# A two-layer macaron kernel: earlier weight loads in borrowed buffers, a halved broadcast, and a new order table

## What is computed

```python
x = x + 0.5 * _L0_ffn_ref(_layernorm(x), ...)   # silu(gate) * up, then down; int32 weights minus 128, hidden 704
x = x + _L0_attn_ref(_layernorm(x), ...)        # 16 heads of 16, rotary, causal softmax, output projection
x = x + 0.5 * _L0_ffn_ref(_layernorm(x), ...)
x = x + 0.5 * _L1_ffn_ref(_layernorm(x), ...)   # sigmoid(x1) * x2; weights rounded to -1, 0, 1 by mean(abs(w))
x = x + _L1_attn_ref(_layernorm(x), ...)        # 16 query heads on 4 key heads, ALiBi bias, causal softmax
x = x + 0.5 * _L1_ffn_ref(_layernorm(x), ...)
```

## Time and profile before

| | before |
|---|---|
| median of 3 runs | 582.63 us (580.01, 582.63, 582.76) |
| profiled execution | 580.01 us, its span 578.3 us |
| PE busy | 531.4 us |
| DVE, ACT, POOL busy | 460.7, 400.1, 341.1 us |
| DMA moved | 31.75 MB, mean 55 GB/s |

### The profile page before, as it was taken

How to read it: one execution, slowest core, us unless ns; L and a number is a source line. 1 busy time by engine, 2 the same in 40 slices (tenths; PEclk the granted TensorE clock), 3 DMA queues, 4 the chain that set the end, 5 groups by cost and what they waited for, 6 DMA issues and landing times.

```text
span 578.3 us, 12694 instructions
## 1 busy us (share of the span) xinstructions
PE 531.4 (92%) x4924; PEld 291.1 (50%) x4924; DVE 460.7 (80%) x813; ACT 400.1 (69%) x605; POOL 341.1 (59%) x427
## 2 busy tenths in 40 slices
PE   2885987998999999999999999999999999999997
PEld 1352643544564564555546455465465644554664
DVE  4799779998799779589986988878898677884453
ACT  5883557597567849766597775878668686679533
POOL 2367858882896687854456284365462845246544
PEclk9997988999999999999999999999999999999999
DMA  8700101121112001130100120010211002111201
GB/s 329 315 2 0 38 18 56 56 75 28 34 70 82 25 16 38 41 116 15 61 21 3 62 76 2 21 49 11 69 41 37 6 22 88 41 38 41 76 36 37
DMA packets 20524, 31.75 MB, mean 55 GB/s; under 512 B 7360, under 2 KB 8768, under 8 KB 20312
## 3 DMA queue, kind: packets, MB, share of 16 engines
q1 hardware_dynamic: 20464, 30.94, 15.2%
HBM read 13.75 MB, written 2.36 MB: 28 GB/s over the span
## 4 chain that ended last, share of the span: by engine, by line
PE 57%; DVE 15%; POOL 6%; ACT 6%; SPq 5%; issue 5%; DMA 4%; DVEq 0%; POOLq 0%; ACTq 0%
PE PS L584 16%; PE PS L608 10%; PE PS L695 10%; PE PS L675 5%; PE PS L626 5%; PE PS L660 4%; DVE MX L1049 4%; PE PS L710 3%; ACT PB L837 3%; DMA MASKM<-maskm 2%; PE PS L568 2%; SPq L519 2%; PE PS L642 2%; PE PS L540 2%; POOL PB L1153 1%
## 5 line engine op out<-in xcount | busy, mean ns | idle before, releaser
L837 ACT ACTIVATE PB<-PS 128x1024 f32<-128x1024 f32 x160 | 157.7, 1023 | 44.4 <-PE PS L675 40.7
L1049 DVE TENSOR_REDUCE MX<-PS 128x2 f16<-128x1024 f32 (+2 forms) x192 | 157.1, 864 | 18.4 <-PE PS L540 18.0
L584 PE MATMUL PS<-XT,WGU 128*128 128x512 f16 x660 | 158.4, 384 | 4.3 <-DVE DS L1010 2.8
L1125 POOL TENSOR_TENSOR HH<-TH,HH 128x512 f16<-128x512 f32 x71 | 83.1, 1185 | 68.5 <-ACT HH L805 68.5
L1153 POOL TENSOR_SCALAR_AFFINE_SELECT PB<-PB 128x512 f32<-128x512 f32 (+1 forms) x140 | 73.0, 551 | 64.6 <-ACT PB L837 64.4
L584 PEld LDWEIGHTS PS<-XT,WGU 128*128 128x128 f16 x660 | 59.7, 98 | 79.9 <-issue 8.2
L608 PE MATMUL PS<-WD,HH 128*128 128x256 f16 x660 | 77.5, 273 | 0.9 <-POOL HH L1125 0.6
L695 PE MATMUL PS<-PB,V 128*32 128x512 f32 (+3 forms) x1024 | 75.5, 435 | 1.2 <-POOL PB L1153 1.0
L608 PEld LDWEIGHTS PS<-WD,HH 128*128 128x128 f16 x660 | 62.3, 98 | 13.3 <-issue 2.6
L660 PE MATMUL PS<-SK,SQ 63*128 63x256 f16 (+3 forms) x512 | 59.5, 300 | 7.7 <-DVE MX L1049 3.7
L805 ACT ACTIVATE HH<-TH 128x512 f16<-128x512 f32 (+1 forms) x86 | 52.2, 627 | 18.5 <-DVE TH L992 7.0
(11 more groups left out here) (115 smaller groups left out, 751.9 us busy)
## 6 DMA issues: line engine op xcount, KB each, us to landing
SQ<-QPB SPq DMA_DIRECT2D x24, 256.0 KB, 2.5
OC<-OT SPq DMA_DIRECT2D x16, 256.0 KB, 2.4
RB<-scratch SPq DMA_DIRECT2D x64, 64.0 KB, 2.3
SK<-QPB SPq DMA_DIRECT2D x12, 256.0 KB, 2.4
SQ<-MT SPq DMA_DIRECT2D x128, 1.0 KB
out<-X SPq DMA_DIRECT2D x8, 256.0 KB, 2.2
PB<-gu SPq DMA_DIRECT2D x2, 704.0 KB, 6.1
LATE<-gu SPq DMA_DIRECT2D x2, 704.0 KB, 13.8
```

The lines of the kernel that those rows point to most:

```text
L584: m = e.matmul(o[:, :], WGU[l][:, k, col:col + P], rows_of(f)[j][:, k, :], start=j == 0 and k == 0, stop=j == 1 and k == 1)
L837: e.activation(PB[Q % 2][:, j, :, :], two_banks("s", i), ACT.Exp, scale=0.25).then_inc(a_exp, 1)
L1049: e.tensor_reduce(mx[:, :, pr, t], o[:, :, col:col + (t + 1) * P], AX.X, ALU.max, negate=True).then_inc(a_max, 1)
L1125: e.tensor_tensor(hh[1][:, s * T:(s + 1) * T], value_of(j)[0], hh[0][:, s * T:(s + 1) * T], ALU.subtract).then_inc(f_lo, 1)
```

## The change

Six edits come together.

1. LATE is gone. Its contents lie in SQ[1] and SK[1], the stacked tiles of the odd attentions, which are not needed before attention 1.
2. SP issues the layer-1 FFN weights (wd1, then gu1) ahead of batches 2 and 3 of x, the rotary table and the masks.
3. ACT's last four `k` steps (which fill SQ[1] and SK[1]) wait for the end of w14.
4. `R` is two DMAs of 128 KB (the even and the odd partitions) where it was four of 64 KB.
5. The builder's default replaces `dynamic_dma_scratch_size=256`.
6. All five strings of `ORDER` and `banks` are new. Each string has the same letters as often as before.

```diff
-        LATE = sb("LATE", [P, 2, 4 * T])
...
-        late = [LATE[:, k, :] for k in range(2)]
+        late = [t[1][:, :, :].rearrange("p h t -> p (h t)").bitcast(F32) for t in (SQ, SK)]
...
             e.dma_start(BO[:, :], bo1).then_inc(l_a0, 16)
+            e.dma_start(rd[0], wd1[:, 0:4, :]).then_inc(l_w3, 16)
+            e.dma_start(rd[1], wd1[:, 4:, :]).then_inc(l_w3, 16)
+            for k in range(2):
+                e.dma_start(rgu[k], gu1[:, k, :]).then_inc(l_w1, 16)
             e.dma_start(X[:, 2 * NT:, :], x_in[:, 2 * NT:, :]).then_inc(l_x23, 16)
             e.dma_start(ROPE[:, :, :], rope).then_inc(l_c2, 16)
             e.dma_start(MASKW[:, :, :, :], maskw).then_inc(l_c2, 16)
             e.dma_start(MASKM[:, :, :, :], maskm).then_inc(l_c2, 16)
-            e.dma_start(rd[0], wd1[:, 0:4, :]).then_inc(l_w3, 16)
-            e.dma_start(rd[1], wd1[:, 4:, :]).then_inc(l_w3, 16)
-            for k in range(2):
-                e.dma_start(rgu[k], gu1[:, k, :]).then_inc(l_w1, 16)
...
                     src = scratch[n % 2, u].rearrange("(a g s) t -> a g (s t)", a=4, g=2)
-                    for a in range(4):
-                        e.dma_start(RB[32 * a:32 * a + 32, u, :], src[a].unsqueeze(0).to_broadcast([16, 2, T])).then_inc(t_si[u], 16)
+                    for g in range(2):
+                        e.dma_start(RB[g:P:2, u, :], src[:, g, :].unsqueeze(1).to_broadcast([4, 16, T])).then_inc(t_si[u], 16)
...
                     w.wait_ge(l_c2, 48)
+                    if z == 1:
+                        w.wait_ge(p_dve, 30)
...
     "sp":
-        "kkrkrrkDrSrRDSRrrDkkSrRrDSRrrkDrSlkRDSRrkrkrDrrSlRDSRrkkrrDSrDRSrRrkkrDrSRDrSRrDrkkSRrDSRrrOODrSRDSR"
+        "kkrrkrkrDSrRDSRrkrDSRkrrDSRrrDrkSRkDSRrrlkkrDrSRrDSlRrkrkDrSRrDSrRrkkrDrSRDrSRrDrkrkSRDrSRrrrDSRDOSOR"
```

More of the change, by code:

```diff
@@ new lines @@
+        "smsgssmGspmsgsmGmmpsmsmsmgssGmmmpsmsvsvmssmuummmpqqsoooossddssmqmqpsmttdmsdssmgggsGGgpmmgsmGsmssmmgs"
+        "GmmmGpmssvvsmuudsddmdsqmsqoopmottossmgsqsmgmggGGGsgmspmsmgGssGqttpssdgsssdgddGgpgGgmvmmmgmvGuGmuGmoo"
+        "oomqmsqsmsqdmmsdmdsmdmssmmspmssmmsmsttspgssmggmGgGgsmGGgGmspsmstddtddmssggmpmvmgGguusGGsqgsmqsmgGsqm"
+        "sGoomspmmddddmsmsoomspmmttsssggGssGsgmmpsmgGmsgmsmGgGmpmsvsmssmmmdddmsdsspsmsttomogmsguguooGqqqsGmms"
+        "gmGsGggGmspsmmmddmsdssmdmsspsmmssmmspttvsmmgggGgGGgGgGsmmssttssddddooommmopspuusmgqsmqqssggGsGsspssm"
@@ new lines @@
+        "gmmmGpmgvmmgGmGmsmtsmsstsmmpdddmsdooosmgsosmsmgGgGmsmpmsgssGsgsgsspssGGttpddgddgGgGgGggGGoooodddttdg"
+        "ggGgGGgGGgdddd",
+    "dve":
+        "NwNtthwwhwkhwhwhtwthwwNhhwwdwNdwhnhwhkuuhtpqptqdwdpqhnpqhhkuuhhhpqttqpmmmmmxmmmspqsmhpmqxhmdmsmmdmxm"
+        "mkmhsmhnmxsmhmmmcmmxsmmmhmcxmmumummpqpoqoxNmqdppmqmtcmtdmsxhnskhsshmmmmhmmsxshmmhmmcuxumdmdNpqmqopmt"
+        "tomxNhmmphqhkmhmmxhhtqptcshsddnkhsshcmsmmmmhsumxhuhmoommllmlmxmdmmdmmxNmmmmmttNxmhchkhmhmhmhxmdttdmn"
+        "mssmhmsckuuhxhshmlsmhslmhmlomxmddmNmmmoxmttNhchmmkmhhmxmhmhmmmcxmmmdmdnmttmmxshusuoohlklslhmmmxshshs"
+        "mhmmmdmcxmdmNmmmmNttmcxmhhkhhhhmmtxdtdnommomNuumlmxhllchkhmmmmhmxmmhmmmhcxmmtmtdmdomxhomNmhkmmhmxhch"
+        "httcddhhkhhhhooNXtthdkhhhhhddd",
@@ new lines @@
+    "act":
+        "TwwXxxwttthXtthxxhhwhtwhkttwwwthwhXtkhwxthYwyyhthXxkQQvtkthQtvYQtyytthhxxhhQTkQkktthkeeeteeQeeQhhoee"
+        "eteeeoetehhhoeeeteeYoeevecveeyyhcoeQeQeeeXoexxQeQetetehttohheeetheteYohcehveeyvyeeceXoxxQeeeetttQhXe"
+        "hehttoheeethQxhxoeeetQteechtothhtvYtyvchyhhQeQeeQeeeeeoeeXexxeeoeetthththetXhtheheoexxceettoYhtvyyet"
+        "ehQetQhetechehhQeoeeXoexxeeetteeehhteothetehhtXhoeveeeceeecoexxeYteytyhtQQhQeehtetthehheoeeeeeoeeeXe"
+        "oxxecXttvhhtththhteheexexceYeooyyetQXeQQeetteheeoeethothvhthceeeeexhoxceeteeetthXhehoteeeeheeteteeho"
+        "hxxotthchthtcthhthXxxthttthhhthth",
@@ new lines @@
+        "7246102742462135643560256460362350162460642104630516247620432064715640624057216052416204346023406472"
+        "0420620460246024762174026503273462154260264124340631426402635402705402602752406320634613624036024623"
+        "4604750260420720542056024104640264062047142426204672064073410315706426147205674214624064124624606240"
+        "6206450126402375421376024603264060162406314625420760256027024206526045621640365026402605620735207604"
+        "702460362720462412062742043047672650476143571367262737530657065431",
```

43 lines of the change are left out of this document (10 added, 33 removed).

## The result

| | before | changed |
|---|---|---|
| median of 20 runs each, on the same chips | 580.82 us (578.52 to 582.76) | 583.84 us (582.37 to 585.89) |
| ratio to before, 95% interval | | 1.0054 (1.0041 to 1.0066) |
| profiled span | 578.3 us | 584.2 us |

A forecast was written before the change was run, and what follows sets the result against it. PE was taken as the bound, busy 531.4 of 578.3 us. Start -4.5, R +1.5 and other order 0 gave -3.0 us: 577.0 against the profiled execution, 579.6 us against the median; range 573.5 to 587.5 us.

The forecast's parts named there:

- The start, -4.5: Up to the first scores: they come at 86 to 87 us, not 90.8, gaining 4.5 us (between -1 and -6).
- 2.0 us at w13 from the wait for x: In DVE's start: its 2.98 us wait for x is filled with wd1 sums, 2.0 us kept at w13 (0 to 2.98).
- PE's wait of 6.5 us still there: Sign for the start: PE still waits 6.5 us, but the wait ends near 56 us.
- The gain travels to the end unless the order wastes it: After the start: with no DVE slack up to 200 us and none on PE later, the 4.5 us reach the end.
- R, +1.5 (0 to 8.4): R transfers POOL waits for: on four DMA engines each lands about 1.2 us later, costing 1.5 us in all.
- two prices: Cost of one R, estimated from two transfer rows: 13.8 or 11.0 engine-us, so 2.8 to 3.4 us on four engines.
- Rival B: R transfers: R spreads over 16 engines and lands 1.2 us earlier, -8.1 us in all, 574.5 us; chance 0.10.
- A: R transfers decide: all POOL waits for R pass on, plus four moved c, +8.7 us, 591.3 us; chance 0.12.
- The rest of the tables. I take 0, between -3 and +4: Order from 200 us on and the tail: most steps move one or two places, taken as 0 us.
- Rival D: From 200 to 550 us: the new order doubles PE's idle time, +8.0 -3.0, 587.6 us; chance 0.10.
- Rival C: First 200 us: 3 us of the start's gain is lost again after 91 us, 581 to 583 us; chance 0.24.

The follow-up runs named there:

- e3: The kernel before with the new loads, buffers, ACT wait and strings only up to the first scores, old strings behind, old R: 577.35 us, 0.9923 of before.
- e15: The kernel before with the new loads, borrowed buffers, ACT's wait and scratch size, all old strings and the old R: 1.0119 of before, 6.9 us slower.
- e4: The kernel before with its old start and old R, but the new strings behind the first scores: 1.0111 of before, 6.5 us slower.
- e13: e12 with one more change, the transposes t18 write PSUM bank 0 and not bank 2: 582.55 us in a single run, made for its trace.
- e12: The changed kernel with the old four-transfer R and one ACT exponential moved ahead of a norm near 350 us: 1.0015 of before.
- e14: The changed kernel with the old R and t18 in PSUM bank 0, ACT's exponential left behind the norm: 583.20 us in a single run, for its trace.

## Why the prediction was wrong

*The start, -4.5: right in size, by a sum whose terms were partly wrong, so in part luck.* It is 4.5 us in e3's median (2.8 to 6.2), first scores and first maximum within 0.7 us of the forecast. But I had 2.0 us at w13 from the wait for x and nothing from POOL's moved steps. The rows of the changed kernel:

```profile
49.15 0.57 DVE L952 TENSOR_SCALAR SQ<-SQ,GS 128x704 f16<-128x704 f32 x1
49.64 0.58 DVE L952 TENSOR_SCALAR SK<-SQ,GS 128x704 f16<-128x704 f32 x1
50.14 0.94 DVE L956 SCALAR_TENSOR_TENSOR WGU<-SQ,GS 128x704 f16<-128x704 f32 x1
51.00 0.94 DVE L956 SCALAR_TENSOR_TENSOR WGU<-SQ,GS,SK 128x704 f16<-128x704 f32 x1
```

w13 starts 2.35 us later than before and is done 2.3 us earlier: 2.8 us instead of 7.45. I had read in the earlier trace rows that POOL's 3.46 us step stood there, and that the change moves it away, without asking what it did to the DVE step beside it. It is the order and not the new buffers: in e15, with the new buffers and the old order, w13 takes 7.46 us (53.22 to 60.68), as before. No run moves POOL's steps alone, so how much of the 4.5 us they bring is not measured. "PE's wait of 6.5 us still there" was wrong too: PE's longest wait between 20 and 60 us is 2.9 us, at 30.8.

*"The gain travels to the end unless the order wastes it": right.* e3 shows the first half and e4 the second.

*R, +1.5 (0 to 8.4): mechanism right, somewhat small.* Four engines, +0.8 us each on the mean in the old order (expected 0.7 to 1.3), 1.9 to 2.5 us at the end. Of its two prices one was misread: the row of 0.43 for 2.00 us holds 196 KB (98 GB/s) of the 262 that an R moves. The other, 11.0 engine-us from a transfer whose row is whole, held: the changed kernel's R takes 0.23 x 16 x 3.20 = 11.8. Rival B is out (share 0.23), and so is A.

*"The rest of the tables. I take 0, between -3 and +4": the step that failed.* It measured +5.1 us in the changed kernel (3.2 to 7.0) and +6.5 (4.8 to 8.1) behind the old start, both above its upper bound of +4, though the first interval reaches below it. With it at zero the forecast was -3.0; with +5.1 the same sum gives +2.1, and with R at 2.5 the measured 3. It was the term without a row behind it: I wrote that most steps move by one or two places, and took small moves for harmless, though the same prediction says that with 8.0 us of idle in 350 "a new order can mostly lose there". Rival D named this with 0.10, and called for 5.9 us of new idle; in the trace there are 4.3, 3.8 of them without the new R. The order at 350 us, and the bank that `t18` shares with `p17`, stood in the two tables beforehand. What is shown is that the strings behind the first scores lose it, and in which four stretches; the step by step cause is shown for one wait of 1.09 us, and stays open for the rest.

*Rival C (lost from 91 to 200 us): small.* The changed kernel loses 2.1 us between 115 and 193 us, but e3 with the old order loses 1.6 there too, and still ends 4.5 us ahead by the medians.

## What to carry over

When an order changes as a whole, split it at a point where both versions have done the same work, and time each part under the other; here a gain of 4.5 us and losses of 5.1 and 2.5 showed as one small difference. Ask what each joint costs by itself. Give no zero to reordered steps in a stretch where the bounding engine is full: count which of its waits are 0.2 to 0.5 us now, and look who frees the PSUM bank of each moved step. In a DMA, look at the outermost count of both sides before merging transfers: here half the issues left a quarter of the engines.

## What the runs showed of the hardware

**A DVE step held up by POOL.** With the new buffers and the old order (e15), DVE and then POOL:

```profile
53.22 0.59 DVE L951 TENSOR_SCALAR SQ<-SQ,GS 128x704 f16<-128x704 f32 x1
53.72 3.43 DVE L951 TENSOR_SCALAR SK<-SQ,GS 128x704 f16<-128x704 f32 x1
```

```profile
53.31 3.46 POOL L1089 TENSOR_TENSOR WA<-OT,WA 128x1536 f16<-128x1536 f32 x1
```

Two equal DVE instructions take 0.59 and 3.43 us. The first began before POOL's, the second ends 0.4 us behind the end of POOL's step of 3.46 us (56.77). In the changed kernel the same two take 0.57 and 0.58, with nothing longer than 1.46 us on POOL; there POOL's big step stands at 30.11 us and takes 3.11. A profile counts such a held step as busy time of DVE, not as a wait. The Trainium skill ("SBUF — State Buffer", "SBUF: two separate sides") describes a port pair that GpSimd shares with DVE for some kinds of DVE operations, and that the one that starts first holds for its whole instruction; these rows agree, though none shows to which kind this DVE step belongs.

**The clock fell in the middle of the kernel.** Stretches of PE in e13 (busy, granted clock):

```profile
354.00:357.00 3.00, 2.10 (x26) 1.00 0.00 0
357.00:358.00 1.00, 0.75 (x8) 1.00 0.35 125
358.00:359.00 1.00, 0.80 (x7) 0.66 0.43 156
359.00:360.00 1.00, 1.00 (x3) 0.50 0.01 1
```

PE had worked in short groups with gaps of 0.2 to 0.8 us since 354 us, 70 to 80% busy. Then, at 358.3 us, the granted clock fell from 1.00 (2.4 GHz) to 0.50 (1.2 GHz) until 361.7, and `p` to `p` took 1.5 us more than in e12, 1.4 of it in the 12 matmuls named above. e12 and e14 stood longer in one piece at the same place (1.09 and 1.99 us) and kept 1.00; from 354 to 359 us PE of e12 was busy for 3.66 us and that of e13 for 3.65. I can't say from these runs which pattern makes it fall, nor whether a second run of e13 would show it again.

**The clock in the start is chance in part.** 95 to 100 us in the changed kernel, then in its repetition:

```profile
95.00:100.00 5.00, 4.48 (x16) 1.36 (x17) 5.00 (x9) 4.62 (x7) 2.68 (x3) 0.50 0.01 2
```

```profile
95.00:100.00 5.00, 4.89 (x20) 1.56 (x20) 5.00 (x10) 4.66 (x7) 2.26 (x2) 0.66 0.01 2
```

The same instructions: the first trace stands at 0.50 (1.2 GHz) for all of the 5 us and for 6.8 us in all (94.6 to 101.5), the second for 3.4 us (95.2 to 98.6), which gives 0.66 on the mean. By 115 us the two traces differ by 1.6 us.
